# Layer with attention and experts on one core: first fills through seven PSUM banks, the last store awaited later, expert rows fetched over four groups

## What is computed

```python
xn = _layernorm(x)
# attention
q, k, v = split(xn @ qkv_w.T)              # 16 heads of 64
q, k = _rope(q, c, s), _rope(k, c, s)      # t1*c - t2*s, t1*s + t2*c
kb = -p * jnp.log1p(a * dist)
attn = jax.nn.softmax(einsum('bhqd,bhkd->bhqk', q, k) * SCALE + kb[None], axis=-1)
y = einsum('bhqk,bhkd->bhqd', attn, v).reshape(Bb, Ss, H * D) @ out_w.T
# experts
gate = jax.nn.softmax(xr @ Wg); idx = jnp.argmax(gate, axis=1)
h = jax.nn.relu(jnp.einsum('ecm,emf->ecf', dispatched, w1))   # 256 slots for each of 16 experts
expert_out = jnp.einsum('ecf,efm->ecm', h, w2)
combined = expert_out[idx, loc] * (gates_s * valid)[:, None]
return x + y + combined
```

## Time and profile before

| | us |
|---|---|
| median of three timed runs | 1271.6 |
| the three runs | 1269.08, 1271.6, 1276.42 |
| the profiled execution | 1268.28 |
| its span, from the first to the last instruction | 1266.5 |
| mean granted clock of TensorE, as a share of 2.4 GHz | 0.959 |

### The profile page before, as it was taken

One profiled execution on the slowest core, in us unless ns is written; L12 is line 12 of the kernel. 1 busy time (PEld: TensorE's weight loads), 2 busy tenths in 40 slices (PEclk: granted clock), 3 DMA queues, 4 the chain that ended last, 5 costly groups with the idle time before them and its releaser, 6 DMA issues.

```text
span 1266.5 us, 35475 instructions
## 1 busy us (share of the span) xinstructions
PE 1096.5 (87%) x14436; PEld 798.3 (63%) x14436; DVE 1016.0 (80%) x2061; ACT 1002.6 (79%) x1987; POOL 818.2 (65%) x481
## 2 busy tenths in 40 slices
PE   5740799999479999999999998999999999999874
PEld 5730688898146666666666765666666666666653
DVE  7873799997468788878878887887998788788872
ACT  2684688885169889889889897888998898899991
POOL 3035100000279888898889788888888888888741
PEclk9985799999899999999999999999999999999997
DMA  8715576762126556656755584676567557555573
GB/s 259 273 48 206 182 240 226 236 228 103 33 43 126 110 101 122 131 90 114 131 122 94 114 143 89 102 130 122 102 102 155 98 98 130 127 97 101 111 122 75
DMA packets 390289, 165.79 MB, mean 131 GB/s; under 512 B 340722, under 2 KB 380671, under 8 KB 390128
## 3 DMA queue, kind: packets, MB, share of 16 engines
q1 hardware_dynamic: 377856, 143.26, 53.2%
q0 software_dynamic: 4352, 12.41, 2.9%
q10 hardware_dynamic: 7920, 7.87, 2.0%
HBM read 58.79 MB, written 21.00 MB: 63 GB/s over the span
## 4 chain that ended last, share of the span: by engine, by line
PE 38%; DMA 12%; POOL 9%; ACT 6%; issue 5%; DVE 3%; SPq 1%; another core or an unknown queue 1%; POOLq 0%; ACTq 0%
PE ps_x L1303 9%; PE ps_s L1347 8%; PE ps_o L1378 7%; PE ps_t L1358 6%; PE ps_x L1322 5%; DMA pt_dma<-prob_parts 5%; DMA ot<-ctx_parts 4%; ACT prob L1114 3%; PE ps_x L1313 3%; POOL rot L989 2%; DMA res<-in_L_attn_x_dram 2%; POOL prob_parts L999 2%; POOL got L1016 1%; POOL ctx_parts L1007 1%; ACT pt_pe L1098 1%
## 5 line engine op out<-in xcount | busy, mean ns | idle before, releaser
L1224 DVE CUSTOM_DVE_ANT_0 prob<-ps_s,strips,score_scale 128x512 f32<-128x512 f32 x512 | 360.3, 746 | 10.1 <-PE ps_s L1347 9.4
L1114 ACT ACTIVATE prob<-prob,neg_max 128x512 f32<-128x512 f32 x512 | 364.1, 714 | 2.1
L999 POOL TENSOR_TENSOR prob_parts<-prob,prob_parts 128x1024 f16<-128x1024 f32 x128 | 273.3, 2135 | 84.5 <-ACT prob_parts L1104 84.3
L1230 DVE SCALAR_TENSOR_TENSOR pt_pe<-ps_t,pt_pe 128x1024 f16<-128x1024 f32 x128 | 156.0, 1219 | 54.3 <-ACT pt_pe L1098 54.3
L1347 PE MATMUL ps_s<-parts 32*128 32x512 f16 x3072 | 194.7, 383 | 0.2
L1303 PE MATMUL ps_x<-xcur,wqkv_hi 128*128 128x512 f16 x512 | 156.7, 388 | 36.8 <-ACT proj L1076 20.6
L989 POOL TENSOR_TENSOR rot<-prods 128x1024 f32<-128x1024 f32 x62 | 146.5, 2363 | 12.2 <-DVE parts L1267 11.7
L1358 PEld LDWEIGHTS ps_t<-ident,prob 128*128 128x128 f32 x1024 | 109.8, 141 | 64.0 <-issue 40.2
L1358 PE MATMUL ps_t<-ident,prob 128*128 128x128 f32 x1024 | 139.8, 279 | 8.2 <-DVE pt_pe L1230 8.2
L993 POOL TENSOR_TENSOR parts<-rot,parts 128x1024 f16<-128x1024 f32 x62 | 132.6, 2139 | 6.3 <-ACT parts L1093 6.3
L1104 ACT CAST prob_parts<-prob 128x1024 f16<-128x1024 f32 x128 | 133.7, 1044 | 2.0
(11 more groups left out here) (190 smaller groups left out, 2600.0 us busy)
## 6 DMA issues: line engine op xcount, KB each, us to landing
raw<-in_L_ffn_w_dram SPq DMA_DIRECT2D x32, 1024.0 KB, 5.1
xa<-in_L_attn_x_dram SPq DMA_DIRECT2D x8, 512.0 KB, 6.5
xt_dram<-xth SPq DMA_DIRECT2D x8, 512.0 KB, 5.1
slots_dram<-zeros SPq DMA_DIRECT2D x4, 1024.0 KB, 8.3
xa<-slots_dram SPq DMA_DIRECT2D x16, 256.0 KB, 5.3
expert_dram<-xa POOLq DMA_DIRECT2D x16, 256.0 KB, 6.8
xcur<-xt_dram SPq DMA_DIRECT2D x8, 512.0 KB, 4.3
res<-in_L_attn_x_dram ACTq DMA_DIRECT2D x8, 512.0 KB, 4.0
```

The costliest lines, as they stand in the source:

```text
L999: nc.gpsimd.tensor_tensor(prob_parts[:, n % 2, 1], prob[:, (2 * n + 1) % 3], prob_parts[:, n % 2, 0], ALU.subtract).then_inc(prob_lo, 1)
L1114: nc.scalar.activation(prob[:, s % 3, q, :], prob[:, s % 3, q, :], ACT.Exp, bias=neg_max[:, 2 * (s % 3) + q:2 * (s % 3) + q + 1], scale=-1 ...
L1224: nc.vector.tensor_tensor_reduce(prob[:, s % 3, q, :], ps_s[u][:], strips[:, HG * j + u, start:start + S], score_scale[:, 0:1], 3.0e38, AL ...
L1230: nc.vector.scalar_tensor_tensor(out=pt_pe[:, n % 2, 1].rearrange("p q k c -> p q (k c)"), in0=ps_t[:], scalar=P_SCALE, in1=pt_pe[:, n % 2 ...
```

## The change

Three things are changed.

First, the first fills go to seven banks: the four score banks ps_s, the two halves of ps_t, and ps_x. Seven of them stand ahead of the first scores, the other five behind these in quad 0 (the values 1 of group 0, the values of group 1, the keys of group 1). A fill of the later five waits only for its own bank. The rotation of the queries of group 0 is added on GpSimd (rotate_queries), that of the keys on VectorE. The keys of group 1 are multiplied on VectorE into prods1, which is the memory of pt_dma; so the first two DMA transposes wait for the rotation of these keys. ScalarE's copy and GpSimd's product for them are gone.

Second, GpSimd doesn't wait for the stores at the end of `experts`, but in `attention`, ahead of the first gather. ctxt and got are allocated earlier and thus lie elsewhere.

Third, got has four tiles instead of two, each half with a semaphore of its own. The gathers of a batch stand at the end of groups 0 and 1 of the batch before, the combines at the end of groups 2 and 3. The routes are loaded in quad 2 instead of quad 5.

```diff
@@ experts, GpSimd
             over_experts(store)
-            for r in range(2):
-                pool.wait_ge(o_stored[r], 16 * (E // 2))
@@ attention
+        FIRST_FILLS = [(0, "qk", 0), (0, "qk", 1), (0, "qk", 2), (0, "qk", 3), (1, "qk", 0), (1, "qk", 1), (0, "v", 0),
+                       (0, "v", 1), (1, "v", 0), (1, "v", 1), (1, "qk", 2), (1, "qk", 3)]
+        BEFORE_SCORES = 7
+        spare = [ps_t[:, 0, :], ps_t[:, 1, :], ps_x[:]]
+        first_banks = [p[:] for p in ps_s] + [spare[i % 3] for i in range(len(FIRST_FILLS) - HG)]
-        FIRST_FILLS = [(F, "qk", i) for F in range(2) for i in range(4)] + [(F, "v", i) for F in range(2) for i in range(2)]
@@ SyncE
                 sp.wait_ge(prob_lo, n + 1)
+                if n < 2:
+                    sp.wait_ge(rotated, 3)
...
-                if q == 5 and b < NB - 1:
+                if q == 2 and b < NB - 1:
                     load_routes(b + 1)
@@ GpSimd, group
                 prob_low(4 * g)
-                if b == 0 and j == 0:
+                if g == 0:
+                    rotate(1, 1, FIRST_FILLS.index((1, "qk", 3)) + 1)
+                    combine(0, 0)
+                    low(1, 1)
                     combine(0, 1)
-                if b < NB - 1 and j:
-                    if j > 1:
-                        combine(b + 1, j - 2)
-                    if j < 3:
-                        gather(b + 1, j - 1)
                 if F:
                     rotate(F, 0, fills_before(b, 8 * j) + 2)
...
                 context_lo(2 * g)
-
+                if b < NB - 1:
+                    if j < 2:
+                        gather(b + 1, j)
+                    else:
+                        combine(b + 1, j - 2)
+
+            rotate_queries()
+            for r in range(2):
+                pool.wait_ge(o_stored[r], 16 * (E // 2))
             gather(0, 0)
             rotate(1, 0, FIRST_FILLS.index((1, "qk", 1)) + 1)
+            gather(0, 1)
             low(1, 0)
-            multiply(1, FIRST_FILLS.index((1, "qk", 2)) + 1)
-            rotate(1, 1, FIRST_FILLS.index((1, "qk", 3)) + 1)
-            low(1, 1)
-            combine(0, 0)
-            gather(0, 1)
@@ ScalarE
             def quad(n, b, q):
+                if n == 1:
+                    high(1, 1)
...
                 exponentials(n, 0)
+                if n == 0:
+                    read_val(0, 1, FIRST_FILLS.index((0, "v", 1)))
                 exponentials(n, 1)
+                if n == 0:
+                    read_val(1, 0, FIRST_FILLS.index((1, "v", 0)))
+                    read_val(1, 1, FIRST_FILLS.index((1, "v", 1)))
+                    high(1, 0)
@@ VectorE, quad
-                read_fill(b, 2 * q)
+                if n:
+                    read_fill(b, 2 * q)
                 negate(n, j, t, 3)
+                if n == 0:
+                    read_val(0, 1)
+                    read_val(1, 0)
+                    read_val(1, 1)
+                    read_q(1, 2, prods1)
+                    read_q(1, 3, prods1)
+                    read_fill(b, 2 * q)
@@ TensorE
-                wait(pe, x_free, fill)
+                bank = ps_x[:]
+                if fill < len(FIRST_FILLS):
+                    bank = first_banks[fill]
+                    if fill >= HG + 3:
+                        pe.wait_ge(x_free, fill - 2)
+                else:
+                    pe.wait_ge(x_free, fill)
...
                 scores(n, q % TPB)
+                if n == 0:
+                    for i, (F, what, k) in enumerate(FIRST_FILLS[BEFORE_SCORES:], BEFORE_SCORES):
+                        fill((what, k, F), 0, 0, i)
```

118 lines of the change are left out of this document (61 added, 57 removed).

## The result

The changed kernel takes 1237.0 us as the median of four runs (1232.6 to 1238.4), the kernel before 1271.7. The ratio is 0.972, with a 95% interval of 0.968 to 0.976. The forecast was 1234, its range 1221 to 1247. The profiled run of after is its fastest, 1232.55 us with a span of 1230.8.

What follows compares the result with a forecast made beforehand. TensorE was taken to set the pace, so only its waits could give time. From 1268.3 us: minus 14 (start), 27 (quad 10), 5 (reciprocal), plus 8 (loads), 3 (later prob_low) gives 1233.3; 1 allowed makes 1234, range 1221 to 1247.

## What to carry to other kernels

On a queue that issues slow transfers in order, what counts is not how long a small load takes but which transfer stands behind it and how much slack that one's user has: two loads of 2 KB cost 8 us here, and loading all of them once ahead of the stage made the kernel 10 to 14 us faster. A buffer with more tiles, made so that instructions can move, can also take a wait on one's own engine away (6 of the 24 us of quad 10 here); try that step alone first and measure. When a wait goes, look one quad later before booking the gain, and when a term of the sum comes out right, test its cause all the same. When the profile calls what ended a wait "remote", look up in the program which semaphore it was and who raises it, before two instructions that merely start together are taken for cause and effect; and before a kernel's trace is set against one from another session, look whether the effect exists in that session at all.
